# A fused macaron block: x normalised on ScalarE, its first low half through a product on TensorE, and a new order of all queues

## The chip, the cores and the metric

One core of a Trainium2 chip. The metric is the time of one execution on the device in microseconds; three runs of the kernel before gave 164.55, 164.68 and 165.19, median 164.68.

## What is computed

x has 1024 rows of 256 channels. A block of three residual steps, each on a layer-normalised copy of its input:

```python
x = x + 0.5 * ffn(layernorm(x), gate_w, up_w, down_w, gate_scale, up_scale, down_scale)
x = x + attn(layernorm(x), w_qkv, w_g, w_proj, gn_weight, gn_bias)
x = x + 0.5 * ffn(layernorm(x), ...)              # the same weights again

def ffn(h):                                       # weights rounded to float8_e4m3fn
    gate = silu((h @ q8(gate_w)) * gate_scale)    # 256 -> 768
    up = (h @ q8(up_w)) * up_scale
    return ((gate * up) @ q8(down_w)) * down_scale

def attn(h):                                      # 16 heads of 16 channels
    q, k, v = split(h @ w_qkv); q, k = xpos(q), xpos(k)
    y = (q @ k.T * decay_mask / 4) @ v            # no softmax
    return (silu(h @ w_g) * groupnorm(y)) @ w_proj
```

## The kernel before

Rows are worked on in 8 tiles of 128 (`NT`). In the two feedforward steps four tiles make a group of 512 columns (`GT`), and the 768 inner channels are six blocks: 12 gate/up products per step, numbered `j`; `PRODUCTS` orders those of the first step as blocks 0 to 2 of both groups, then 3 to 5 of both. Attention runs over 8 chunks of 128 rows with a running state.

There are no loops at run time. Each engine has one queue, written out by hand as calls of small functions, and engines meet only at semaphores; a function waits for what it reads and for the buffer that it writes. An instruction that waits holds up all behind it on its engine.

**Opening.** SyncE loads x in three parts (tiles 0 and 1, 2 and 3, 4 to 7) between the pieces of the weights. `tile_stats` and `mean_var` (VectorE) give mean and variance, `roots` (GpSimd, L309) the power -1/2 for a group of tiles, `shift_rows` (VectorE) minus mean times root. Even tiles are normalised by `norm_act` (ScalarE, L409) from that shift, odd ones by `norm_tile` (VectorE, L680). `turn_h` (TensorE, L1089) transposes four tiles into two PSUM banks. `split_h` (ScalarE, L417) copies a bank, scaled by 2^-90, to `hhi` in fp32r (a high half), and `rest_h` (VectorE, L692) writes what is lost, bank times 2^-90 minus `hhi`, to `hlo`. Products take both halves: `gate_up(j)` is four 128x512 matmuls for gate and four for up (L1125), `first_gate_up` the same for j = 0 (L1101). `keep_busy` are products of zeros.

**Weights.** Each of 8 pieces is rounded by `grid_step` (L613), `grid_clip` (L619), `grid_add` (L625) on VectorE, `subtract` on VectorE (L630) or GpSimd (L305, where `SUB_ON_POOL` names it), and `to_weights` (ScalarE, L401). Three buffers (`GRID_SLOTS`) are shared by turns. `PIECES_NEEDED` says how many pieces a product waits for; `down(0)` needs the seventh, its second half the eighth.

**First feedforward step.** Per product: `silu` (ScalarE, L427), `fuse_up` (VectorE, L709: up times scale times silu), `split_f` (ScalarE, L435) and `rest_f` (VectorE L717 or GpSimd L320, where `REST_ON_POOL` names it) give `fhi` and `flo`; `fuse` has four slots. `down(d)` multiplies them with the down weights for tile d (L1153), `scale_down` and `add_down` give x1. `turned_vectors` (VectorE) copies the scales that TensorE has transposed, `half_scale` halves the down scales.

**Attention, chunk c.** `norm_tile`, `turn_h2` (L1169), `copy_h2`; `project_qk` (L1181) and `project_vg` (L1192, L1195); `rotate_parts` (VectorE, L746) and `rotate` (L758, L759); `turn_qk` (L1207) and `copy_qk` (ScalarE: kT, qM, qT); `scores` (L1224) into four banks, `mask_scores(c, 0..3)` (VectorE, L766); `update_state` (L1261), `mask_kv`, `add_state`; `values` (L1240 and L1248); `copy_y`, `turn_y` (L1281), `group_mean` (L786, L790), `square` (ScalarE, L484), `group_var` (L798), `group_roots` (GpSimd, L336), `group_norm` (L804), `turn_gn` (L1294), `affine` (ScalarE, L492), `gated` (L812), `project_out` (L1304), `add_proj` (L816). `turn_qk(c+1)` and `turn_h2(c+2)` write banks of the scores of chunk c, so they wait for its first and second mask; `scores(c+1)` waits for all four, `values(c)` for each in turn.

In a full chunk TensorE's order is scores(c), project_out(c-3), project_vg(c+1), turn_h2(c+2), turn_gn(c-2), values(c), turn_y(c-1), turn_qk(c+1), update_state(c+1), project_qk(c+2). The last chunk is interleaved with the first products of the second feedforward step, whose second group (`turn_h(3)`) needs the last tile of the attention's output.

## Time and profile before

| | |
|---|---|
| runs | 164.55, 164.68, 165.19 us; median 164.68 |
| profiled execution | 164.07 us, span 162.3 us, mean granted TensorE clock 1.00 (2.4 GHz) throughout |
| chain that ended last, by engine | TensorE 62%, VectorE 16%, GpSimd 9%, issue 7%, DMA 2% |

The span runs from the first to the last instruction; 1.8 us of the execution lie around it. How to read the profile: PE is TensorE (its weight loads are PEld), DVE is VectorE, ACT ScalarE, POOL GpSimd, SP SyncE. An instruction's row gives its start, its length, engine, line, operation, output and inputs. The length of an instruction that waits for a port inside the engine includes that wait. Ends of matmuls are modelled, so that neighbours overlap in the rows: what a group takes from the queue is read from its start to the next one's.

### The profile page before, as it was taken

How to read it: one execution, taken by the hardware profiler on the slowest of the kernel's cores; microseconds unless marked ns; L12 is line 12 of the kernel's file. 1: busy time of each engine (PE TensorE's matmuls, PEld its weight loads, DVE VectorE, ACT ScalarE, POOL GpSimd, SP SyncE). 2: the span in 40 equal slices, each digit the busy share in tenths (PEclk: the TensorE clock that was granted, in tenths of full speed). 3: DMA queues.
4: the chain of work that ended last, by engine and by line, in shares of the span. 5: the costliest groups of instructions: out<-in, count | busy, mean ns of one | idle time of the engine just before them, and what ended most of it. 6: DMA issues, size and time to landing. Idle time of an engine off the chain costs nothing.

```text
span 162.3 us, 3236 instructions
## 1 busy us (share of the span) xinstructions
PE 151.5 (93%) x1111; PEld 117.6 (72%) x1111; DVE 134.0 (83%) x295; ACT 71.4 (44%) x158; POOL 70.5 (43%) x77
## 2 busy tenths in 40 slices
PE   5758699999999999999999999999999989999992
PEld 2335478787979785858686786668778768888991
DVE  1899799997787694879898999999898989657774
ACT  3235669953232214152608071354716718554300
POOL 2558569851376300256372737373567630000000
PEclk9999999999999999999999999999999999999999
DMA  4999501903000000000000000000000000000123
GB/s 111 288 306 338 203 2 24 360 7 129 2 0 4 0 0 4 0 0 0 6 0 0 6 0 0 4 0 2 4 0 2 4 0 0 0 0 0 67 69 129
DMA packets 6864, 8.41 MB, mean 52 GB/s; under 512 B 432, under 2 KB 5568, under 8 KB 6848
## 3 DMA queue, kind: packets, MB, share of 16 engines
q1 hardware_dynamic: 6848, 8.20, 15.1%
q8 instruction: 9, 0.15, 0.4%
q14 instruction: 7, 0.06, 0.1%
HBM read 7.15 MB, written 1.05 MB: 51 GB/s over the span
## 4 chain that ended last, share of the span: by engine, by line
PE 62%; DVE 16%; POOL 9%; issue 7%; DMA 2%; ACT 1%; SPq 1%; POOLq 0%; DVEq 0%
PE bank L1125 14%; PE bank L1153 12%; PE bank L1181 9%; POOL grstd L336 5%; PE bank L1224 4%; PE bank L1248 4%; PE bank L1192 3%; PE bank L1304 3%; PE bank L1195 3%; DVE flo L717 3%; DMA xt<-in_L_attn_x 2%; PE bank L1207 2%; PE bank L1261 2%; DVE raw L625 2%; POOL rstd L314 2%
## 5 line engine op out<-in xcount | busy, mean ns | idle before, releaser
L1125 PE MATMUL bank<-hh,gate_r 128*128 128x512 f32 x92 | 25.7, 401 | 0.2
L1125 PE MATMUL bank<-hh,up_r 128*128 128x512 f32 x92 | 25.7, 401 | 0.0
L1153 PE MATMUL bank<-down_r,fhi 128*128 128x256 f32 x96 | 24.2, 291 | 0.4 <-DVE flo L717 0.4
L336 POOL TENSOR_TENSOR grstd<-gve,neg_half 128x16 f32<-128x16 f32 x8 | 23.3, 2915 | 0.8 <-POOL gve L332 0.2
L1153 PE MATMUL bank<-down_r,flo 128*128 128x256 f32 x96 | 23.4, 282 | 0.0
L435 ACT ACTIVATE fhi<-fuse 128x512 fp32r<-128x512 f32 x24 | 14.8, 631 | 15.5 <-DVE fuse L709 15.5
L766 DVE TENSOR_TENSOR sc<-bank,msk 128x512 f32<-128x512 f32 x32 | 20.6, 682 | 0.6 <-PE bank L1224 0.6
L1125 PEld LDWEIGHTS bank<-hh,gate_r 128*128 128x128 f32 x92 | 16.8, 188 | 4.6 <-issue 1.2
L1125 PEld LDWEIGHTS bank<-hh,up_r 128*128 128x128 f32 x92 | 16.7, 189 | 4.2 <-issue 0.8
L709 DVE SCALAR_TENSOR_TENSOR fuse<-bank,vec,gact 128x512 f32<-128x512 f32 x24 | 17.6, 747 | 2.5 <-ACT gact L427 1.3
L427 ACT ACTIVATE gact<-bank,vec 128x512 f32<-128x512 f32 x24 | 16.1, 681 | 7.3 <-PE bank L1125 5.8
L1153 PEld LDWEIGHTS bank<-down_r,fhi 128*128 128x128 f32 x96 | 18.1, 189 | 1.3 <-DVE flo L717 0.8
L1153 PEld LDWEIGHTS bank<-down_r,flo 128*128 128x128 f32 x96 | 18.1, 189 | 0.5 <-issue 0.2
L312 POOL TENSOR_SCALAR ve<-mv 128x1 f32<-128x1 f32 (+3 forms) x15 | 4.4, 293 | 29.4 <-DVE mv L652 29.4
L492 ACT ACTIVATE ga<-bank,vec 128x128 f32<-128x128 f32 x16 | 6.5, 455 | 23.2 <-PE bank L1294 23.2
L1181 PE MATMUL bank<-wqkv,h 128*128 128x512 f32 x32 | 15.3, 599 | 0.0
L717 DVE TENSOR_TENSOR flo<-fuse,fhi 128x512 fp32r<-128x512 f32 x19 | 14.9, 794 | 0.1
L305 POOL TENSOR_TENSOR grid<-raw,grid 128x768 f32<-128x768 f32 (+2 forms) x6 | 10.5, 1763 | 7.7 <-DVE raw L625 7.7
L729 DVE TENSOR_TENSOR yd<-bank,ds 128x256 f32<-128x256 f32 x16 | 6.8, 423 | 7.4 <-PE bank L1153 7.3
L314 POOL TENSOR_TENSOR rstd<-ve,neg_half 128x1 f32<-128x1 f32 (+3 forms) x15 | 10.8, 721 | 1.3
L1304 PE MATMUL bank<-wp,go 128*128 128x256 f32 x32 | 8.8, 398 | 0.5 <-DVE go L812 0.4
L1224 PE MATMUL bank<-qM,kT 32*128 32x256 f32 x128 | 9.2, 400 | 0.0
(86 smaller groups left out, 279.7 us busy)
## 6 DMA issues: line engine op xcount, KB each, us to landing
raw<-in_rotation SPq DMA_DIRECT2D x1, 1536.0 KB, 6.7
out<-xt SPq DMA_DIRECT2D x8, 128.0 KB, 1.7
raw<-in_L_ffn_down_w SPq DMA_DIRECT2D x2, 384.0 KB, 7.7
wqkv<-in_L_attn_w_qkv SPq DMA_DIRECT2D x1, 768.0 KB, 9.1
xt<-in_L_attn_x SPq DMA_DIRECT2D x2, 256.0 KB, 3.3
xt<-in_L_attn_x SPq DMA_DIRECT2D x1, 512.0 KB, 5.9
raw<-in_rotation SPq DMA_DIRECT2D x1, 512.0 KB, 3.4
raw<-in_L_ffn_gate_w SPq DMA_DIRECT2D x1, 384.0 KB, 6.4
```

The source lines that it names most:

```text
L314: pool.tensor_tensor(rstd[:, a:b], ve[:, a:b], neg_half[:, 0:b - a], ALU.pow).then_inc(rstd_done, 1)
L336: pool.tensor_tensor(grstd[:, c % 2], gve[:, :], neg_half[:, :], ALU.pow).then_inc(grstd_done, 1)
L427: nc.scalar.activation(gact[:, j % 2, :], pairs[j // (NG * NI)][j % 2][0][:, :], ACT.Silu, scale=gate_col[:, i:i + 1]).then_inc(silu_done, 1)
L435: nc.scalar.activation(fhi[:, g % NG, i, :], fuse[:, j % FUSE_SLOTS, :], ACT.Copy).then_inc(fhi_done, 1)
L709: dve.scalar_tensor_tensor(out=fuse[:, j % FUSE_SLOTS, :], in0=pairs[j // (NG * NI)][j % 2][1][:, :], scalar=up_col[:, i:i + 1], in1=gact[ ...
L717: dve.tensor_tensor(flo[:, g % NG, i, :], fuse[:, j % FUSE_SLOTS, :], fhi[:, g % NG, i, :].bitcast(F32), ALU.subtract).then_inc(flo_dve, 1)
L766: dve.tensor_tensor(sc[:, r].rearrange("p k m t -> p (k m) t"), b_sc[r][:, :].rearrange("p (g t) -> p g t", t=P), causal.unsqueeze(1).to_b ...
L1125: mm = pe.matmul(dst[:, :], wr[m][:, k * I + i * P:k * I + (i + 1) * P], half[:, k, g % NG, :], start=(k == 0 and half is hhi), stop=(k == ...
L1153: mm = pe.matmul(downs[d][:, 0:C], half[:, g % NG, i, t * P:(t + 1) * P], wr["down"][:, i * C:(i + 1) * C], start=(i == 0 and half is fhi) ...
L1181: mm = pe.matmul(b_qk[:, :], h2[:, c % 2, k, :], wqkv[:, k, 0:2 * C], start=(k == 0), stop=(k == KC - 1))
L1224: mm = pe.matmul(b_sc[r][:, k * C:(k + 1) * C], kT[at, k, :], qM[at, k].rearrange("p m t -> p (m t)"), start=True, stop=True)
L1304: mm = pe.matmul(b_gn[c][:, C:2 * C], go[:, k, :], wp[:, k, :], start=(k == 0), stop=(k == KC - 1))
```

## The change

The opening: all eight tiles of x are normalised on ScalarE. For the first group the low half is no longer the work of VectorE. TensorE adds the product of a negated unit matrix (times 2^90, made by ScalarE from the unit matrix) with `hhi` to the transposed tiles in their bank, so that the bank holds x minus the high half, and ScalarE copies that to `hlo` (`low_h`). `first_gate_up` goes by k, with `take_high` ahead of each high product. `turned_vectors` and `half_scale` go from VectorE to ScalarE. `subtract(0)` and `subtract(6)` go to GpSimd and `subtract(3)` to VectorE; `rest_f` 0, 1, 2 and 11 go to VectorE and 3, 9 and 10 to GpSimd. `qT` gets a second buffer.

The order of every queue is new. In a full chunk of the attention TensorE's is scores(c), project_out(c-3), project_vg(c+1), turn_h2(c+2), update_state(c), turn_qk(c+1), turn_gn(c-2), project_qk(c+2), turn_y(c-1), values(c), and then scores(c+1). `down(7)` goes behind `scores(1)`, `project_vg(0)` ahead of `project_qk(0)`. In the last stretch `values(7)` comes two steps after `scores(7)` and `project_out(7)` one gate/up pair later.

```diff
+NORM_ON_ACT = [0, 1, 2, 3, 4, 5, 6, 7]
-SUB_ON_POOL = [1, 2, 3, 4, 5, 7]
+SUB_ON_POOL = [0, 1, 2, 4, 5, 6, 7]
-REST_ON_POOL = [0, 1, 2, 4, 11]
+REST_ON_POOL = [3, 4, 9, 10]
...
         @block.gpsimd
             roots(0)
+            subtract(0)
             roots(1)
             subtract(1)
             subtract(2)
-            subtract(3)
             roots(2)
             subtract(4)
-            rest_f(0)
             subtract(5)
-            rest_f(1)
-            rest_f(2)
+            subtract(6)
+            rest_f(3)
             rest_f(4)
             subtract(7)
...
         @block.scalar
+            def low_h(g, k):
+
+                act.wait_ge(high_taken, KC * g + k + 1)
+                nc.scalar.activation(hlo[:, k, g, :], turn[g][k][:, :], ACT.Copy, scale=H_SCALE).then_inc(hlo_done, 1)
...
+            to_weights(0)
             norm_act(0)
-            to_weights(0)
+            norm_act(1)
             norm_act(2)
+            negative_ident()
+            norm_act(3)
             split_h(0, 0)
+            turned_vectors()
+            to_weights(1)
             split_h(0, 1)
-            to_weights(1)
+            low_h(0, 0)
+            low_h(0, 1)
             to_weights(2)
             silu(0)
             to_weights(3)
             norm_act(4)
+            norm_act(5)
             norm_act(6)
+            norm_act(7)
             silu(1)
...
         @block.vector
             grid_clip(1)
-            norm_tile(1)
-            subtract(0)
             grid_step(2)
-            norm_tile(3)
+            shift_rows(1)
             grid_clip(2)
             grid_step(3)
-            shift_rows(1)
+            grid_add(1)
             grid_clip(3)
-            grid_add(1)
             grid_add(2)
             grid_add(3)
-            rest_h(0, 0)
             tile_stats(4)
-            rest_h(0, 1)
-            mean_var(4)
             tile_stats(5)
             tile_stats(6)
+            mean_var(4)
             tile_stats(7)
             mean_var(5)
             mean_var(6)
             mean_var(7)
-            turned_vectors()
+            subtract(3)
             grid_step(4)
             grid_step(5)
+            shift_rows(2)
             grid_clip(4)
-            shift_rows(2)
-            norm_tile(5)
-            norm_tile(7)
+            grid_clip(5)
             grid_add(4)
-            grid_clip(5)
+            grid_add(5)
             fuse_up(0)
...
             for c in range(2, 5):
-                mask_kv(c)
                 group_var(c - 2)
                 rotate_parts(c + 1)
                 mask_scores(c, 0)
                 mask_scores(c, 1)
-                mask_scores(c, 2)
+                rotate(c + 1)
                 if c >= 3:
                     add_proj(c - 3)
                 group_norm(c - 2)
+                mask_kv(c)
+                mask_scores(c, 2)
                 mask_scores(c, 3)
-                rotate(c + 1)
                 norm_stats(NT + c + 3, NT + c + 4)
+                gated(c - 2)
                 group_mean(c - 1)
-                gated(c - 2)
                 norm_tile(NT + c + 3)
...
         @block.tensor
+            def take_high(g, k):
+
+                pe.wait_ge(minus_done, 1)
+                pe.wait_ge(hhi_done, KC * g + k + 1)
+                pe.matmul(turn[g][k][:, :], minus[:, :], hhi[:, k, g, :], start=False, stop=True,
+                          skip_group_check=True).then_inc(high_taken, 1)
```

## Rows read from the trace of the kernel before

**Rows 1.** The page, part 1: busy time, share of the span and instructions.
```profile
PE 151.5 (93%) x1111; PEld 117.6 (72%) x1111; DVE 134.0 (83%) x295; ACT 71.4 (44%) x158; POOL 70.5 (43%) x77
```

**Rows 2.** Busy time by stretch: window, length, each engine (instructions), clock, DMA.
```profile
28.00:40.00 12.00, 11.65 (x62) 9.57 (x61) 11.06 (x16) 7.58 (x12) 6.37 (x5) 1.00 0.47 171
```

**Rows 3.** Timeline of the opening: start, length, instruction [idle before, releaser].
```profile
15.00 1.07 POOL L312 TENSOR_SCALAR ve<-mv 128x4 f32<-128x4 f32 x1 [0.57 <-DVE mv L652]
...
17.62 1.09 ACT L409 ACTIVATE h<-xt,shift,rstd 128x256 f32<-128x256 f32 x2 [1.28 <-DVE shift L637]
...
18.36 1.06 PE L1089 MATMUL bank<-msk,h 128*128 128x128 f32 x8 [1.23 <-ACT h L409]
...
22.32 1.10 PE L1125 MATMUL bank<-hh,up_r 128*128 128x512 f32 x4
```

**Rows 4.** Groups by form: count, busy us, mean ns of one, idle before.
```profile
L336 POOL TENSOR_TENSOR grstd<-gve,neg_half 128x16 f32<-128x16 f32 x8 | 23.3, 2915 | 0.8 <-POOL gve L332 0.2
...
L766 DVE TENSOR_TENSOR sc<-bank,msk 128x512 f32<-128x512 f32 x32 | 20.6, 682 | 0.6 <-PE bank L1224 0.6
...
L692 DVE SCALAR_TENSOR_TENSOR hh<-bank,hh 128x512 fp32r<-128x512 f32 x8 | 5.2, 684 | 0.0
...
L484 ACT ACTIVATE gsq<-gd 128x256 f32<-128x256 f32 x8 | 3.4, 426 | 2.7 <-DVE gd L790 2.7
...
L680 DVE TENSOR_SCALAR h<-xt,mv,rstd 128x256 f32<-128x256 f32 x4 | 1.6, 411 | 0.1
```

**Rows 5.** Timeline of GpSimd and VectorE where both read SBUF.
```profile
26.25 2.00 POOL L320 TENSOR_TENSOR flo<-fuse,fhi 128x512 fp32r<-128x512 f32 x1
...
27.03 1.77 DVE L717 TENSOR_TENSOR flo<-fuse,fhi 128x512 fp32r<-128x512 f32 x1
...
34.07 0.69 DVE L717 TENSOR_TENSOR flo<-fuse,fhi 128x512 fp32r<-128x512 f32 x1
...
34.23 2.23 POOL L305 TENSOR_TENSOR grid<-raw,grid 128x768 f32<-128x768 f32 x1 [2.29 <-DVE raw L625]
...
35.33 1.69 DVE L717 TENSOR_TENSOR flo<-fuse,fhi 128x512 fp32r<-128x512 f32 x1
```

**Rows 6.** Timeline of TensorE ahead of the second half of down(0).
```profile
35.89 1.10 PE L1125 MATMUL bank<-hh,gate_r 128*128 128x512 f32 x4
36.83 1.10 PE L1125 MATMUL bank<-hh,up_r 128*128 128x512 f32 x4
38.28 0.39 PE L1153 MATMUL bank<-down_r,fhi 128*128 128x256 f32 x1 [0.35 <-DVE flo L717]
```

**Rows 7.** Timeline of TensorE: two holes, and the same steps in a full chunk.
```profile
68.88 0.66 PE L1207 MATMUL bank<-msk,rot 128*128 128x128 f32 x4
69.67 0.68 PE L1261 MATMUL bank<-v,rot 128*128 128x128 f32 x4
...
74.93 0.38 PE L1169 MATMUL bank<-msk,h 128*128 128x128 f32 x2
75.58 0.44 PE L1294 MATMUL bank<-msk,gn 128*128 128x128 f32 x2 [0.26 <-DVE gn L804]
...
84.37 0.38 PE L1169 MATMUL bank<-msk,h 128*128 128x128 f32 x2
84.59 0.38 PE L1294 MATMUL bank<-msk,gn 128*128 128x128 f32 x2
...
86.67 0.60 PE L1207 MATMUL bank<-msk,rot 128*128 128x128 f32 x4
87.18 0.68 PE L1261 MATMUL bank<-v,rot 128*128 128x128 f32 x4
```

**Rows 8.** Timeline of TensorE: the scores of chunks 4 and 5.
```profile
89.51 1.15 PE L1224 MATMUL bank<-qM,kT 32*128 32x256 f32 x16
...
98.46 1.15 PE L1224 MATMUL bank<-qM,kT 32*128 32x256 f32 x16
```

**Rows 9.** Timeline of TensorE: the last projection of the attention.
```profile
130.88 1.13 PE L1304 MATMUL bank<-wp,go 128*128 128x256 f32 x4 [0.43 <-DVE go L812]
```

More of the change, by code:

```diff
@@ L83, in rests, with norms @@
     return n - on_pool, on_pool
-def normed_until(n):
-    return (n + 1) // 2 if n < NT else n + 1 - NT // 2
+def norms(n):
+    on_act = sum(t < n for t in NORM_ON_ACT)
+    return n - on_act, on_act
 def products_until(g, i):
@@ L1337, in _ @@
             down(4, 0, NI // 2)
+            project_vg(0)
             project_qk(0)
+            turn_h2(1)
             down(5, 0, NI // 2)
-            project_vg(0)
-            turn_h2(1)
             down(4, NI // 2)
             down(5, NI // 2)
+            down(6)
             turn_qk(0)
-            down(6)
             project_qk(1)
-            update_state(0)
-            down(7)
             scores(0)
@@ L1351, in _ @@
             turn_h2(2)
+            update_state(0)
             turn_qk(1)
+            project_qk(2)
             values(0)
-            project_qk(2)
             scores(1)
+            down(7)
+            turn_qk(2)
+            turn_h2(3)
+            update_state(1)
             turn_y(0)
-            update_state(1)
             project_vg(2)
-            turn_h2(3)
             values(1)
-            turn_qk(2)
-            update_state(2)
             project_qk(3)
+            scores(2)
             for c in range(2, 5):
-                scores(c)
                 if c >= 3:
@@ L1369, in _ @@
                 turn_h2(c + 2)
+                update_state(c)
+                turn_qk(c + 1)
                 turn_gn(c - 2)
+                project_qk(c + 2)
+                turn_y(c - 1)
                 values(c)
-                turn_y(c - 1)
-                turn_qk(c + 1)
-                update_state(c + 1)
-                project_qk(c + 2)
-            scores(5)
+                scores(c + 1)
+            update_state(5)
+            project_vg(6)
+            turn_h2(7)
             project_out(2)
-            project_vg(6)
+            project_qk(7)
             turn_gn(3)
-            turn_h2(7)
             turn_qk(6)
             turn_y(4)
-            project_qk(7)
             values(5)
+            scores(6)
+            update_state(6)
             project_out(3)
-            scores(6)
+            turn_qk(7)
             project_vg(7)
             turn_gn(4)
-            update_state(6)
-            turn_qk(7)
+            values(6)
             turn_y(5)
-            values(6)
+            scores(7)
             c, j0 = NT - 1, NG * NI
@@ L1396, in _ @@
             turn_y(c - 1)
-            scores(c)
+            values(c)
             project_out(c - 3)
+            turn_y(c)
             gate_up(j0, ("gate",))
             gate_up(j0, ("up",))
-            values(c)
+            turn_gn(c - 2)
             gate_up(j0 + 1, ("gate",))
-            turn_y(c)
-            turn_gn(c - 2)
             gate_up(j0 + 1, ("up",))
+            turn_gn(c - 1)
+            project_out(c - 2)
             gate_up(j0 + 2, ("gate",))
-            turn_gn(c - 1)
-            gate_up(j0 + 2, ("up",))
-            project_out(c - 2)
-            gate_up(j0 + 3, ("gate",))
             project_out(c - 1)
             turn_gn(c)
+            gate_up(j0 + 2, ("up",))
+            gate_up(j0 + 3, ("gate",))
+            project_out(c)
             gate_up(j0 + 3, ("up",))
-            project_out(c)
             gate_up(j0 + 4, ("gate",))
             gate_up(j0 + 4, ("up",))
+            turn_h(3)
             gate_up(j0 + 5, ("gate",))
-            turn_h(3)
             gate_up(j0 + 5, ("up",))
-            down(NT, 0, NI - 2)
             gate_up(j0 + 6, ("gate",))
```

357 lines of the change are left out of this document (189 added, 168 removed).

## The prediction

> **What bounds the kernel now.** I read the shares of busy time first: TensorE is busy 93% of the span, VectorE 83%, ScalarE 44%, GpSimd 43% [rows 1]. An average hides stages, so the table by stretch comes next: from 28 to 40 us TensorE has 11.65 of 12.00 us and VectorE 11.06 [rows 2]. From about 19 us on the kernel is a TensorE queue with a few holes, and VectorE is nearly full beside it. Work taken from VectorE is therefore worth only what it shortens of a hole in the TensorE queue; a reordering can close holes and can also open new ones.
>
> The holes are read from the starts of TensorE's groups, because the modelled ends of matmuls hide short ones. There are four kinds. (a) Before 19 us: TensorE idles 1.23 us until the second half of x is normalised [rows 3]. (b) Ahead of the second half of the first down product: the last gate/up group starts at 36.83 and the down product at 38.28, 1.45 us later, where the group before it took 0.94; about 0.52 us of hole, waiting for `flo` [rows 6]. (c) In the first attention chunks: `turn_qk(2)` at 68.88 to `update_state(2)` at 69.67 is 0.79, against 0.51 for the same step in a full chunk, so 0.28; and `turn_h2(4)` at 74.93 to `turn_gn(0)` at 75.58 is 0.65 against 0.22, so 0.43, waiting for `gn` [rows 7]. The full chunks run at TensorE's pace, without a hole: `scores(4)` starts at 89.51 and `scores(5)` 8.95 later [rows 8]. (d) In the last stretch: `project_out(7)` at 130.88 has 0.43 of idle time ahead of it, waiting for `go` [rows 9].
>
> **Opening.** The change takes from VectorE four normalisations (0.41 each), the two `rest_h(0, k)` (0.68 each) [rows 4], the three small `vec` instructions and `subtract(0)`; before the second half's statistics end that is about 1 us of its queue on the path, since part of the rest fell into waits for data. It adds to ScalarE four normalisations (two in a row took 1.09, so 0.6 for the first and 0.5 for each behind it), the two `low_h` and the negated unit matrix, and to TensorE two 128x512 products, about 0.23 each, a quarter of a gate/up group [rows 3, 6]. No row shows a ScalarE read of a bank to which an fp32r product has been added to transposes; the nearest are the 0.68 of VectorE's `rest_h`, which reads the same bank, and ScalarE's 0.5 for a tile half as wide; I take 0.6 each, bounds 0.5 and 0.8, hidden either way as follows.
>
> In the first half the new order of ScalarE is `to_weights(0)`, norms 0 and 1, norm 2, the unit matrix, norm 3. With roots and shifts where they are now or up to 0.5 us earlier, the fourth tile is turned between 10.4 and 11.0 us, and everything up to the gate product of `gate_up(2)` ends near 16.5. But none of this is last: `turn_h(1)` waits for tiles 4 to 7. Their statistics end about 1.0 us earlier (13.7 instead of 14.9, just ahead of the 15.00 of the first root instruction). Then two things take back: GpSimd's first instruction after them took 1.07 us, while two VectorE `grid_step`s ran beside it [rows 3], and in the new order `subtract(3)` and the same two steps stand there again; and all four norms stand in one row on ScalarE, four at 0.5 instead of two beside two. I get the shift at 16.45, norms from 16.65 to 18.75, and the last tile turned at 19.05 instead of 19.42 (18.36 and 1.06). `fuse_up(0)` now stands behind `grid_add(5)` on VectorE and ends at 20.0; the second up product waits for it, and `fuse_up(1)` at 21.95 releases the third, at 22.05 instead of 22.32 [rows 3]. So 0.27 us is left of the opening at that point. Bounds: 0.9 if the roots are not held up, 0 if the four norms end where they do now.
>
> **From 22 to 38 us.** The new plan moves `subtract(6)` and other `rest_f`s to GpSimd and takes `rest_f(0)` to `(2)` back to VectorE: VectorE's work between `fuse_up(2)` and `rest_f(8)` comes out nearly the same (two `rest_f` and a `fuse_up` more, a `subtract` and a `grid_add` less). 
>
> Walking the new queues with these prices: `grid_step(6)` waits 0.25 for `subtract(5)`, `rest_f(2)` 0.45 for `subtract(6)`, `grid_step(7)` 1.2 for `rest_f(3)`, `grid_add(7)` 0.45 for `rest_f(4)`, `rest_f(6)` 0.45 for `subtract(7)`: 2.8 us in all, as much as now. `rest_f(8)` ends at 37.9, the down product starts at 38.0 instead of 38.28. **Term 1 is -0.3 us**: the hole (b) goes, part of what the opening won goes with it. Bounds: without any new collision -1.25 (0.75 from the opening and 0.52 from the hole); if GpSimd's `rest_f(4)` slips in between `grid_step(7)` and `grid_clip(7)`, `fuse_up(6)` is 1.2 late, `up(8)` waits, and it is +0.5.
>
> The Trainium skill ("SBUF — State Buffer", who interferes with whom) says the same of the port pair: an exclusive lock, held for a whole instruction, against GpSimd, by VectorE instructions with two SBUF inputs as well as by its fast modes. It speaks against moving `subtract(0)` and `(6)` to GpSimd. The trace agrees for these operations, with the 1.77 and 1.69 above. If the powers (`rstd`) hold the pair for their whole length too, the last `shift_rows` and term 1 move by some tenths, to near 0.
>
> **First chunks.** `project_vg(0)` goes ahead of `project_qk(0)`, `down(7)` behind `scores(1)`, `update_state` one chunk later, `values(c)` directly ahead of `scores(c+1)`. I walked TensorE's new queue against the masks (0.68 each), the two rotation products (the same shape, taken at the same length) and the copies. `turn_qk(2)` has `down(7)` ahead of it and no longer waits: **term 2, -0.3**. `turn_gn(0)` stands 1.1 us further back, behind `update_state(2)` and `turn_qk(3)`, at about 4.2 us after `scores(2)` starts; the mean power of 2.9 us that feeds it has ended by then: **term 3, -0.4** [rows 4, 7]. Bounds for both together: -0.8 and 0.
>
> **Full chunks.** In a chunk that starts with `scores(c)` at S, `group_var(c-2)` at the head of VectorE's queue needs the square, which ScalarE does behind the copy of the values, which now end at S: 0.43 us each [rows 4], so the variance starts at S+0.85, not before S. Behind it wait the two rotation products to S+2.4, masks 0 and 1 to S+3.65, `rotate`, `add_proj` and `group_norm` to S+5.05. TensorE wants the second mask at S+3.80 (`turn_h2`), `rotate` at S+4.5, `gn` at S+5.0. The chunk stays at 8.95, with margins of 0.15 and 0.1. **Term 4, 0**; bounds 0 and +1.0 (0.34 in each of three chunks, if the first half of `rotate` takes twice the 0.33 that I take, beside an addition on GpSimd).
>
> **Last stretch.** `project_out(7)` stands behind one more gate/up pair, which closes (d), 0.43. In exchange `values(7)` has only `turn_h(2)` and `turn_y(6)` (1.25 us) between it and `scores(7)`, where VectorE needs four masks and a variance, 2.7 us or more: about 0.7 of a new hole; the gate product behind it waits 0.5 for `rest_h(2, 1)`, while holes of 0.1 to 0.2 at several places of today's order close. **Term 5, 0**; bounds -0.8 and +1.5. The tail after the last gate/up product is the same.
>
> **The sum**: -0.3 -0.3 -0.4 +0 +0 = -1.0 us. The profiled execution took 164.07 us, 162.3 of it span and 1.8 around it; it becomes 163.1. It lies 0.6 under the median of the runs, 164.68, so the forecast for the median is 163.7.
>
> **Rivals.** (A) As above: 163.7, own range 163.1 to 164.3, chance 0.38. (B) The opening's gain arrives whole, since the collisions fall otherwise than I walked them: term 1 is -1.25, which gives 162.7; for it speaks that the opening takes so much from VectorE; against it, that it is full in [rows 2] and that the four norms stand in a row. Chance 0.22. (C) The GpSimd instruction takes the lock between `grid_step(7)` and `grid_clip(7)`: term 1 is +0.5, the time 164.5; chance 0.20. (D) Slower: what stands behind the values on VectorE comes too late. It has a margin of 0.15 us; beyond it each tenth costs a tenth in each of three chunks, and the same chain runs over the end, where `group_var(3)`, `mask_scores(5, 1)` and `turn_y(4)` wait in a row. Priced at 1.0 (chunks) and the upper bound of term 5 (1.5), minus 0.3 of overlap, it gives 163.7 + 2.2 = 165.9. It decides from about 0.5 us of lateness per chunk. Chance 0.14. (E) The change doesn't do what it says: the negated product doesn't shorten the opening, since ScalarE with its eleven more instructions is last there; terms 2 and 3 stay, 164.0 to 164.3; chance 0.06.
>
> **Chances.** About 0.5% (0.8 us) is what a measurement of this kernel can tell from no change. Under 163.9 lie two thirds of A (0.27), B (0.22) and a little of E: 0.50. Over 165.5 lies D: 0.14. The rest, 0.36, is no difference. The range that leaves 2 in 10 out goes from the middle of B, 162.3, to 165.1, past C.
>
> **What would show it.** Right: the last transpose of `turn_h(1)` ends near 19.0; the first product of the second half of `down(0)` starts at 37.8 to 38.1 with VectorE still full ahead of it; `scores(4)` starts about 1.5 us earlier than 89.51 (0.5 of it because its `update_state` now comes behind it); scores stand 8.95 apart. Wrong: `turn_h(1)` done before 18.6 (B), an `up` product that waits over 0.5 us for `fuse` between 28 and 36 us (C), chunks over 9.3 us (D), or a first half that is turned later than 11.4 (E).

## The result

Before, the runs beside which the changed kernel was timed had a median of 164.22 us (163.32 to 165.86). The changed kernel's median is 162.81 us (162.08 to 164.07): ratio 0.992, 95% interval 0.990 to 0.994, 1.4 us faster. A second timing of the same kernel gave 162.37 us and 0.990 (0.988 to 0.993). The forecast was 1.0 us less than before, 163.7 with a range of 162.3 to 165.1. The profiled spans are 162.3 and 161.0 us, a difference of 1.3. Of all runs named below, one that took 249.46 us at a mean granted clock of 0.57 (order in two halves, first kernel) and one of 165.51 us (its reverse) lie outside and are in no ratio.

From the page of the changed kernel, busy time and the chain that ended last, to be held against [rows 1]:

```profile
PE 152.3 (95%) x1113; PEld 118.8 (74%) x1113; DVE 131.2 (81%) x285; ACT 75.5 (47%) x169; POOL 69.8 (43%) x77
...
PE 73%; DVE 13%; issue 4%; DMA 4%; SPq 3%; POOL 1%; ACT 0%; DVEq 0%; ACTq 0%
```

VectorE has 2.8 us less to do, ScalarE 4.1 more, and TensorE fills 95% of a shorter span. The opening, from the timeline of the changed kernel (start, length, engine, line, instruction, idle time before and what ended it), answers to [rows 3]:

```profile
13.59 1.00 POOL L315 TENSOR_SCALAR ve<-mv 128x4 f32<-128x4 f32 x1 [1.26 <-DVE mv L687]
...
16.15 2.08 ACT L412 ACTIVATE h<-xt,shift,rstd 128x256 f32<-128x256 f32 x4 [1.40 <-DVE shift L672]
16.89 1.83 PE L1102 MATMUL bank<-msk,h 128*128 128x128 f32 x8 [1.38 <-ACT h L412]
...
18.71 0.74 DVE L730 SCALAR_TENSOR_TENSOR fuse<-bank,vec,gact 128x512 f32<-128x512 f32 x1
...
20.61 1.09 PE L1148 MATMUL bank<-hh,gate_r 128*128 128x512 f32 x4
...
21.54 1.11 PE L1148 MATMUL bank<-hh,up_r 128*128 128x512 f32 x4
```

`turn_h(1)` ends at 18.72 instead of 19.42, although its four tiles now come one by one, 0.5 apart, and its products are strung over 1.83 us. The third up product (of block 3 in the order of `PRODUCTS`, `up(3)`) starts at 21.54 instead of 22.32: the opening brought 0.78 there. From 27 to 38 us part of it was lost. The same timeline:

```profile
27.61 3.31 POOL L323 TENSOR_TENSOR flo<-fuse,fhi 128x512 fp32r<-128x512 f32 x2
...
28.12 1.66 DVE L648 TENSOR_SCALAR grid<-raw 128x768 uint32<-128x768 uint32 x1
...
29.81 1.53 DVE L654 TENSOR_SCALAR grid<-grid 128x768 f32<-128x768 f32 x1
30.63 1.09 PE L1148 MATMUL bank<-hh,gate_r 128*128 128x512 f32 x4
31.25 0.74 DVE L730 SCALAR_TENSOR_TENSOR fuse<-bank,vec,gact 128x512 f32<-128x512 f32 x1
...
32.14 1.17 PE L1148 MATMUL bank<-hh,up_r 128*128 128x512 f32 x4 [0.42 <-DVE fuse L730]
33.38 1.16 PE L1148 MATMUL bank<-hh,gate_r 128*128 128x512 f32 x4
...
37.90 0.28 PE L1176 MATMUL bank<-down_r,fhi 128*128 128x256 f32 x1
```

GpSimd runs `rest_f(3)` and `rest_f(4)`. VectorE's `grid_step(7)` waits for the first of them (1.66) and `grid_clip(7)`, behind it, for the second (1.53; where nothing runs beside it, 0.55). So `fuse_up(6)` ends at 31.99, `up(8)` starts 1.51 after its gate product instead of 0.93, and the next group 1.24 later instead of 0.94. The hole (b) of [rows 6], 0.52, is gone, and holes of 0.58, 0.30 and 0.06 ahead of 32.14, 33.38 and 34.38 have come. With the same work between, it is 16.36 us from the third up product to the second half of `down(0)`, 15.96 before; that half starts at 37.90, against 38.28.

From there on I compare the starts of the scores. Before, they lie at 56.86, 63.52, 72.00, 80.57, 89.51, 98.46, 108.30 and 115.71; after, at 54.73, 61.63, 70.81, 78.59, 87.48, 96.49, 106.54 and 113.40. `update_state(c)`, 0.52 us, used to stand ahead of `scores(c)` and now stands behind it; from `scores(2)` on the work ahead is otherwise the same. Allowing for it, the lead over before is 0.67 us at `scores(2)`, 1.46 at `scores(3)`, 1.45 at `scores(5)` and 1.3 at the end of the span, and the differences are the terms of the table below. The first full chunk, TensorE, to be held against the rows of a full chunk in [rows 7]:

```profile
73.74 0.38 PE L1192 MATMUL bank<-msk,h 128*128 128x128 f32 x2
73.96 0.61 PE L1284 MATMUL bank<-v,rot 128*128 128x128 f32 x4
...
74.41 0.60 PE L1230 MATMUL bank<-msk,rot 128*128 128x128 f32 x4
74.84 0.38 PE L1317 MATMUL bank<-msk,gn 128*128 128x128 f32 x2
75.06 1.88 PE L1203 MATMUL bank<-wqkv,h 128*128 128x512 f32 x4
```

There is no hole in front of `turn_gn(0)` (0.43 before), and `turn_qk` takes 0.43 from start to next start where it took 0.51. The end, TensorE:

```profile
96.49 1.15 PE L1247 MATMUL bank<-qM,kT 32*128 32x256 f32 x16
...
100.50 0.41 PE L1192 MATMUL bank<-msk,h 128*128 128x128 f32 x2 [0.46 <-DVE sc L787]
...
104.65 0.41 PE L1304 MATMUL bank<-msk,yT 128*128 128x128 f32 x2 [0.51 <-issue]
...
116.16 2.38 PE L1271 MATMUL bank<-sc,v 128*32 128x128 f32 x32
```

Idle times of 0.46 and 0.51 stand between `scores(5)` and `scores(6)`; from start to next start the first hole is 0.63 (1.52 from the second group of `project_vg(6)` to `turn_h2(7)`, 0.89 in a full chunk) and the second about 0.6. `values(7)` takes 2.38 instead of 1.12, since it waits for its masks.

| term | forecast | profiled, after less before |
|---|---|---|
| 1, to the second half of `down(0)` | -0.3 | -0.38 |
| 2, hole at `turn_qk(2)` and its surroundings | -0.3 | -0.29 |
| 3, hole at `turn_gn(0)` and its chunk | -0.4 | -0.79 |
| 4, full chunks | 0 | +0.01 |
| 5, behind `scores(5)` | 0 | +0.15 |
| sum | -1.0 | -1.30 |

### The profile page after: what moved, and what is told of

Its sections match the earlier page's. It is cut to its first block, busy times and chain, and to the rows that moved or that the text cites. A ratio compares the mean times of both kernels' runs of the same rounds, so it can differ in the third digit from the quotient of the medians.

```text
span 161.0 us, 3249 instructions
## 1 busy us (share of the span) xinstructions
PE 152.3 (95%) x1113; PEld 118.8 (74%) x1113; DVE 131.2 (81%) x285; ACT 75.5 (47%) x169; POOL 69.8 (43%) x77
## 4 chain that ended last, share of the span: by engine, by line
PE 73%; DVE 13%; issue 4%; DMA 4%; SPq 3%; POOL 1%; ACT 0%; DVEq 0%; ACTq 0%
PE bank L1148 18%; PE bank L1176 13%; PE bank L1203 9%; PE bank L1271 5%; PE bank L1247 5%; PE bank L1327 5%; PE bank L1215 4%; DMA xt<-in_L_attn_x 4%; PE bank L1218 4%; DVE fuse L730 2%; PE bank L1230 2%; PE bank L1284 2%; PE bank L1263 2%; DVE grid L648 1%; PE bank L1192 1%
## 5 line engine op out<-in xcount | busy, mean ns | idle before, releaser
L1176 PE MATMUL bank<-down_r,fhi 128*128 128x256 f32 x96 | 23.7, 285 | 0.0
L738 DVE TENSOR_TENSOR flo<-fuse,fhi 128x512 fp32r<-128x512 f32 x20 | 14.0, 717 | 3.1 <-ACT fhi L461 3.0
L308 POOL TENSOR_TENSOR grid<-raw,grid 128x768 f32<-128x768 f32 (+2 forms) x7 | 12.0, 1723 | 9.1 <-DVE raw L660 9.1
L468 ACT ACTIVATE h<-bank 128x256 f32<-128x256 f32 x8 | 3.1, 385 | 26.0 <-PE bank L1192 26.0
L315 POOL TENSOR_SCALAR ve<-mv 128x1 f32<-128x1 f32 (+3 forms) x15 | 5.0, 332 | 15.5 <-DVE mv L687 15.5
L347 POOL TENSOR_TENSOR state<-state,kvm 128x256 f32<-128x256 f32 x6 | 4.4, 728 | 15.6 <-DVE kvm L797 13.9
L317 POOL TENSOR_TENSOR rstd<-ve,neg_half 128x1 f32<-128x1 f32 (+3 forms) x15 | 10.3, 687 | 1.2
L1271 PE MATMUL bank<-sc,v 128*32 128x128 f32 x256 | 10.2, 277 | 0.0
```

Source lines behind the costliest of these rows:

```text
L308: pool.tensor_tensor(packed(grid, q), piece(raws[PIECES[q][0]], q), packed(grid, q), ALU.subtract).then_inc(sub_pool, 1)
L317: pool.tensor_tensor(rstd[:, a:b], ve[:, a:b], neg_half[:, 0:b - a], ALU.pow).then_inc(rstd_done, 1)
L738: dve.tensor_tensor(flo[:, g % NG, i, :], fuse[:, j % FUSE_SLOTS, :], fhi[:, g % NG, i, :].bitcast(F32), ALU.subtract).then_inc(flo_dve, 1)
L1176: mm = pe.matmul(downs[d][:, 0:C], half[:, g % NG, i, t * P:(t + 1) * P], wr["down"][:, i * C:(i + 1) * C], start=(i == 0 and half is fhi) ...
L1271: mm = pe.matmul(b_y[r * 2 * D:(r + 1) * 2 * D, k * P:(k + 1) * P], v2[:, c % 2, hd, :], sc[:, r, k, m, :], start=(c == 0 and m == 0), sto ...
```

## The experiments

Eleven new kernels were run, and the changed one again, all beside runs of the kernel before (medians 164.05 to 164.22 us). A distance inside one execution is quoted to 0.01 us; the medians move by a few tenths, for two reasons shown further down: the landing of transfers, and the clock that TensorE was granted. A diff is against the changed kernel where nothing else is said.

**The order in two halves.** First the changed opening and order up to `down(3)`, with the order of before behind it. At the join, VectorE:

```diff
             fuse_up(11)
             norm_tile(NT + 1)
             scale_down(3)
             rest_f(11)
+            mean_var(NT + 2)
             rotate_parts(0)
+            rotate(0)
             scale_down(4)
-            rotate(0)
 ...
```

> The changed kernel's order up to the end of down(3) and the last of the first feedforward step (its opening with the product of the negated unit matrix included), and from there every queue as before (qT keeps its second buffer). Theory (the gain has two independent parts, one of 0.4 us up to the second half of down(0), the rest from the attention's order): 0.3 to 0.5 us faster than before, ratio 0.9970 to 0.9982, and the starts of the scores keep the old distances. Rival (the opening alone carries the gain, what follows only passes it on): 1.0 to 1.4 us faster, ratio 0.992 to 0.994.

Measured: 164.77 us, ratio 1.003 (1.001 to 1.005), no gain at all. The opening is there (`turn_h(1)` ends at 18.86). But the timeline has a wait that neither kernel has:

```profile
46.18 1.27 POOL L323 TENSOR_TENSOR flo<-fuse,fhi 128x512 fp32r<-128x512 f32 x1
...
46.25 1.34 DVE L701 TENSOR_SCALAR h<-x,mv,rstd 128x256 f32<-128x256 f32 x1
47.52 0.41 DVE L750 TENSOR_TENSOR yd<-bank,ds 128x256 f32<-128x256 f32 x1
...
48.08 0.36 PE L1176 MATMUL bank<-down_r,fhi 128*128 128x256 f32 x1 [0.96 <-DVE yd L750]
```

The old order wants `down(5)` early, and its bank is freed by `scale_down(3)`, which in the new order stands behind `norm_tile(9)`; that one waits 0.9 us for GpSimd's `rest_f(10)`. So this kernel says nothing of the opening. It was run again with the two lines exchanged:

```diff
             fuse_up(11)
-            norm_tile(NT + 1)
             scale_down(3)
+            norm_tile(NT + 1)
             rest_f(11)
```

> The kernel with the changed order up to down(3) and the order of before behind it, with scale_down(3) now ahead of norm_tile(9) on VectorE. In the first form of that kernel scale_down(3) stood behind norm_tile(9), which waits for a power on GpSimd, and TensorE waited 0.96 us for it in front of down(5). Theory (the opening is worth its 0.3 to 0.7 us alone, and the join hid it): that wait is under 0.2 us, the span from the end of turn_h(1) is 0.8 to 1.0 us shorter than in the first form (163.1 less 18.86), the ratio to the kernel before is 0.995 to 0.998. Rival (the old order behind is fitted to the old arrival, and the wait shows up in another place): the ratio stays at 1.000 to 1.003 and a wait of 0.5 us or more stands somewhere in the distances of the first four scores. All of the computation is made.

Measured: 163.36 us, ratio 0.994 (0.992 to 0.996), span 161.5. The wait is gone, and from the end of `turn_h(1)` (18.48) to the end of the span it takes 143.0 us instead of 144.2, in the kernel before 142.9. So the whole gain of this kernel lies ahead of that point. The medians differ by 0.69 us, the upper end of the 0.3 to 0.7 of the first theory; the ratio is a little better than its range.

Then the reverse, the old order up to `down(3)` and the new one behind it (its diff is the other half of the change; its opening is that of [rows 3]):

> The kernel before up to the end of down(3), with its opening, and from there every queue as in the changed kernel (second buffer of qT). Theory (independent parts): 0.8 to 1.0 us faster than before, ratio 0.994 to 0.995; scores(2) to scores(3) takes 7.8 us, not 8.57. Rival (the new attention order is worth nothing without the earlier start): no change. Second rival (the parts feed each other): faster than the whole change minus its first part by more than 0.3 us either way.

Measured: 163.41 us, ratio 0.996 (0.994 to 0.999), span 161.4. `scores(2)` to `scores(3)` takes 7.78 us, as expected; the medians differ by 0.64, less than the 0.8 to 1.0 of the theory, the profiled spans by 0.9. The two halves alone are worth 0.6% and 0.4%; together they make the 0.8% to 1.0% of the whole. Within these intervals they add.

**The last stretch.** The changed kernel up to `scores(5)` and `update_state(5)`, and the old order behind. TensorE:

```diff
             update_state(5)
-            project_vg(6)
-            turn_h2(7)
             project_out(2)
+            project_vg(6)
+            turn_gn(3)
+            turn_h2(7)
-            project_qk(7)
-            turn_gn(3)
             turn_qk(6)
 ...
```

> The changed kernel up to scores(5) and update_state(5), and from there every queue as before. In the trace the stretch from scores(5) to the end takes 0.15 us longer in the changed kernel than in the one before (holes at turn_h2(7), turn_y(4) and inside values(7)), so theory (the new end is a small loss): 0.0 to 0.3 us faster than the changed kernel, 1.3 to 1.6 us faster than before. Rival (the new end is fitted to the state in which the new chunks leave the queues): the old end is up to 0.5 us slower than the changed kernel.

Measured: 164.72 us, ratio 1.005 (1.003 to 1.008), the opposite of what I expected. Its timeline:

```profile
98.33 0.41 DVE L819 TENSOR_REDUCE gvar<-gsq 128x16 f32<-128x256 f32 x1
...
99.11 2.91 POOL L339 TENSOR_TENSOR grstd<-gve,neg_half 128x16 f32<-128x16 f32 x1
...
102.06 0.42 DVE L825 TENSOR_TENSOR gn<-gd,grstd 128x256 f32<-128x256 f32 x1 [0.21 <-POOL grstd L339]
...
102.54 0.44 PE L1317 MATMUL bank<-msk,gn 128*128 128x128 f32 x2 [1.97 <-DVE gn L825]
```

The new chunks hand over with `group_var(3)` not yet done; the old end wants `turn_gn(3)` as its third step and waits 1.97 us for a 2.91 us power. From `scores(5)` to the end of the span it takes 66.34 us, in the changed kernel 64.51. Less the one wait it would be 64.37, an estimate: this kernel was not mended at its join as the one above was, so it says that an end belongs to the chunks ahead of it, and does not price term 5.

**The low half on VectorE.** Of the opening's edits, one undone: `hlo` of the first group is again made by `rest_h(0, k)` on VectorE, without the negated matrix and its two products.

```diff
             grid_add(3)
+            rest_h(0, 0)
             tile_stats(4)
+            rest_h(0, 1)
             tile_stats(5)
 ...
-                            take_high(0, k)
+                            pe.wait_ge(hhi_done, k + 1)
```

> The changed kernel, but the low half of the first group is VectorE's again (the two rest_h, the first ahead of tile_stats(4), the second behind it), without the negated unit matrix, the two products and the two copies. Theory (VectorE's chain of tile_stats(4) to (7), roots, shift and then its full queue up to the hole ahead of the up product of block 8 is what the opening is bound by): all of it moves by 0.6 to 0.7 us, the kernel is 0.5 to 0.7 us slower than the changed one. Rival (the collisions with GpSimd between 27 and 31 us swallow the opening's gain, so its parts are worth nothing): within 0.15 us of the changed kernel. What speaks for the rival: the changed kernel had won 0.78 us at the third up product and only 0.38 at the down product.

Measured: 164.43 us, ratio 1.002 (1.000 to 1.004), 1.6 to 2.1 us over the two medians of the changed kernel and not 0.6. Part of it is TensorE's clock. The table by stretch (window, length, busy time of TensorE, its weight loads, VectorE, ScalarE, GpSimd, then granted clock, DMA share, GB/s):

```profile
16.00:18.00 2.00, 0.04 (x1) 0.07 (x2) 1.07 (x4) 0.78 (x2) 0.99 (x1) 1.00 0.99 379
18.00:20.00 2.00, 1.89 (x10) 1.14 (x11) 2.00 (x4) 2.00 (x5) 0.93 (x1) 1.00 0.45 158
20.00:22.00 2.00, 2.00 (x7) 1.51 (x6) 2.00 (x4) 2.00 (x5) 2.00 (x2) 0.51 0.00 0
22.00:24.00 2.00, 2.00 (x8) 1.56 (x7) 1.48 (x3) 0.74 (x2) 1.35 (x1) 0.63 0.00 0
```

TensorE had stood idle for 2.00 us ahead of `turn_h(1)`, and from 20.0 to 23.3 us it was granted the lower of its two levels, 1.2 GHz instead of 2.4: the eight up products from 19.54 took 3.34 us where they take 2.30 in the changed kernel. So the idle time was filled, with all else left as it was:

```diff
+            keep_busy(4)
             turn_h(1)
```

> The earlier kernel whose first low half is made on VectorE, with four products of zeros of 0.27 us each put in front of turn_h(1) on TensorE, where that engine stood idle for 2.00 us from 15.96 to 17.96, and where afterwards the granted clock was 0.51 from 20 to 22 us and 0.63 from 22 to 24. Theory (of the 2 us that the low half on VectorE cost, about 1.6 was the clock, which fell because TensorE had stood idle): the granted clock stays 1.00 from 14 to 26 us, the eight products up of line 1148 take what they do in the changed kernel and not 3.34, gate(3) starts 0.7 to 1.2 us behind its place in the changed kernel and not 2.07, and the span is 161.0 to 161.6. Rival (the low half's own chain on VectorE is what costs 2 us: the products of the second half wait for it): the clock may or may not be 1.00, but the groups stay long by waits, and the span is 162.4 to 162.8. All of the computation is made, and four products of zeros besides.

Measured: 163.78 us, ratio 0.996 (0.994 to 0.999), by the medians 0.65 us better for four products of zeros. The same table of this kernel:

```profile
16.00:18.00 2.00, 2.00 (x10) 1.45 (x8) 1.07 (x4) 0.61 (x2) 1.26 (x2) 1.00 1.02 388
...
20.00:22.00 2.00, 2.00 (x10) 1.42 (x9) 2.00 (x4) 2.00 (x5) 2.00 (x2) 1.00 0.00 0
22.00:24.00 2.00, 2.00 (x10) 1.51 (x9) 2.00 (x4) 1.95 (x4) 1.75 (x1) 1.00 0.00 0
```

The clock stays up, as the theory says; the span is 162.4 and not 161.0 to 161.6, as the rival says. Neither is all of it. Counted from the first `ve`, the third up product starts 9.30 us later without the filling, 7.93 with it and 7.95 in the changed kernel: behind the statistics the clock was the whole difference, 1.4 us at that point. Not all of that reaches the end: from the end of `turn_h(1)` to `scores(0)` it takes 36.63 us without the filling, 35.98 with it and 36.01 in the changed kernel, so 0.65 is left, as in the medians, and the rest went into waits that were there anyway. The single run of the unfilled kernel in which the mean clock stayed at 1.00 took 163.77 us, the median of the filled one. The other part of the loss lies ahead of the statistics: the two `rest_h`, 0.6 each from start to next start, stand in front of the statistics, and `ve` comes at 15.03 instead of 13.59. Of that 1.44, 1.2 is the two instructions; the other 0.2 is what the landings of the weights and of x differ by, below.

**The four norms in a row.** In the changed kernel, norms 5 and 7 on VectorE again:

```diff
-NORM_ON_ACT = [0, 1, 2, 3, 4, 5, 6, 7]
+NORM_ON_ACT = [0, 1, 2, 3, 4, 6]
 ...
             shift_rows(2)
+            norm_tile(5)
+            norm_tile(7)
             grid_clip(4)
```

> The changed kernel with two of the four normalisations of the second group of tiles (5 and 7) on VectorE again, in front of grid_clip(4), the others on ScalarE. Theory (four normalisations in a row on ScalarE, 2.08 us together, set the end of turn_h(1), so halving them brings it forward; but VectorE then hands over the first products later): turn_h(1) ends 0.7 to 1.0 us sooner behind the first normalisation than in the changed kernel (2.57 us from 16.15 to 18.72), gate(3) starts at most 0.3 us sooner, since fuse_up(0) and rest_h(1, *) stand 1.1 to 1.7 us later on VectorE; the ratio is within 0.004 of the changed kernel's. Rival (TensorE's start of the second group is all that counts): gate(3) starts 0.7 us sooner and the kernel is 0.5 us faster than the changed one. All of the computation is made.

Measured: 163.27 us, ratio 0.993 (0.991 to 0.996). Its timeline:

```profile
15.75 1.09 ACT L412 ACTIVATE h<-xt,shift,rstd 128x256 f32<-128x256 f32 x2 [0.77 <-DVE shift L670]
...
16.50 1.07 PE L1102 MATMUL bank<-msk,h 128*128 128x128 f32 x8 [0.68 <-ACT h L412]
...
18.96 0.74 DVE L728 SCALAR_TENSOR_TENSOR fuse<-bank,vec,gact 128x512 f32<-128x512 f32 x1
...
19.85 1.18 PE L1148 MATMUL bank<-hh,up_r 128*128 128x512 f32 x4 [1.36 <-DVE fuse L728]
```

`turn_h(1)` ends 1.82 us behind the first norm instead of 2.57, as expected, and it is worth nothing, less even than the theory allowed (gate(3) at most 0.3 sooner): `fuse_up(0)` stands 0.7 later on VectorE, counted from the first norm, TensorE waits 1.36 us for the bank that it frees, and gate(3) starts 5.12 behind the first norm instead of 4.46. So with these two norms in it VectorE's queue, not the turning of the tiles, is what the opening's path runs through. What moving them brings is under the noise of the medians (0.991 to 0.996 against 0.990 to 0.994); in the traces, counted from the landing of the gate weights (below), `scores(0)` starts 47.17 us behind it here and 46.46 in the second profile of the changed kernel.

**The collision and the masks.** One move on VectorE takes `fuse_up(6)` from behind the pair of waits:

```diff
             grid_step(7)
-            grid_clip(7)
             fuse_up(6)
+            grid_clip(7)
             grid_add(7)
```

> The changed kernel with one step moved: fuse_up(6) on VectorE between grid_step(7) and grid_clip(7), not behind both. In the changed kernel grid_step(7) took 1.66 us and grid_clip(7) 1.53 us instead of 0.55, beside GpSimd's rest_f(3) and rest_f(4), and the up product of block 8 waited for fuse_up(6), which could have run from 29.7. Theory (the hole is made of these two waits for the other engine's whole instruction; fuse_up, with an input in PSUM, passes): fuse_up(6) ends 1.5 us earlier, the hole of 0.5 us ahead of that up product goes, 0.5 to 0.7 us faster than the changed kernel. Rival (VectorE's sum up to rest_f(8) is what binds, and the down product waits for it): the hole moves to down(0), under 0.15 us of gain.

Measured: 161.94 us, ratio 0.987 (0.985 to 0.989). The changed kernel, run beside it, had 162.37. From the end of `turn_h(1)` to `scores(0)` it takes 35.43 us instead of 36.01 in both profiles of the changed kernel, the 0.58 of the hole. The timeline:

```profile
28.06 1.65 DVE L648 TENSOR_SCALAR grid<-raw 128x768 uint32<-128x768 uint32 x1
29.66 0.75 DVE L730 SCALAR_TENSOR_TENSOR fuse<-bank,vec,gact 128x512 f32<-128x512 f32 x1
30.32 0.97 DVE L654 TENSOR_SCALAR grid<-grid 128x768 f32<-128x768 f32 x1
...
31.52 1.10 PE L1148 MATMUL bank<-hh,up_r 128*128 128x512 f32 x4
```

`fuse_up(6)`, with an operand in PSUM, runs its usual 0.75 beside GpSimd's `rest_f(4)`, and the clip pays only the rest of that (0.97 instead of 1.53). Holes of 0.32 and 0.08 stay two and three groups behind `up(8)`, much as the 0.30 and 0.06 of the changed kernel; they are not the work of this pair of waits. Another move takes the hole ahead of `turn_h2(7)` (0.46 idle, 0.63 from start to next start):

```diff
             mask_scores(5, 0)
+            mask_scores(5, 1)
             tile_stats(16)
             mask_kv(5)
             rotate(6)
-            mask_scores(5, 1)
```

> The changed kernel with mask_scores(5, 1) directly behind mask_scores(5, 0) on VectorE, ahead of tile_stats(16), mask_kv(5) and rotate(6). Theory (turn_h2(7) waits for this mask, 0.63 us of hole): the hole goes, turn_y(4) behind it keeps its own of 0.5; 0.4 to 0.6 us faster. Rival (the chain over affine(3) to turn_y(4) or the one over group_roots at the end is as late, and takes it back): under 0.15 us.

Measured: 162.27 us, ratio 0.989 (0.986 to 0.992); `scores(5)` to `scores(6)` 9.40 instead of 10.05. The gain is seen in the trace alone: the median is only 0.1 under the 162.37 of the changed kernel beside it. These two with a third, the variance of chunk 5 behind all four masks of `scores(7)`:

```diff
             mask_scores(c, 0)
-            group_var(c - 2)
             mask_scores(c, 1)
             mask_scores(c, 2)
             mask_scores(c, 3)
+            group_var(c - 2)
```

> The changed kernel with l1's and m1's moves and a third one: group_var(5) behind the four masks of chunk 7, since values(7) stood over these masks for 1.26 us more than in a full chunk. If the moves add: 0.9 to 1.4 us faster than the changed kernel, 2.2 to 2.7 faster than before. If the last stretch is bound by the three powers of 2.9 us in a row on GpSimd: the third move costs up to 0.3.

Measured: 162.98 us, ratio 0.992 (0.990 to 0.995). The first two moves are in it to the hundredth (35.41 and 9.40), and the third costs 1.6, not the 0.3 at most of the second theory: from `turn_h(2)` to `turn_h(3)` it takes 19.62 instead of 18.00. GpSimd, its own timeline:

```profile
116.53 2.92 POOL L339 TENSOR_TENSOR grstd<-gve,neg_half 128x16 f32<-128x16 f32 x1
...
120.05 2.90 POOL L339 TENSOR_TENSOR grstd<-gve,neg_half 128x16 f32<-128x16 f32 x1
...
123.56 2.95 POOL L339 TENSOR_TENSOR grstd<-gve,neg_half 128x16 f32<-128x16 f32 x1
```

Three powers stand in a row, 3.5 apart, and the third releases `turn_gn(7)`. They stand in a row in the changed kernel too, but there the first starts 2.62 us behind `scores(7)`, here 4.41; a late start of the first shifts all three. The hole in `values(7)` that the move was to close hardly shrank (2.16 from start to next start instead of 2.32). Without the third move:

> The changed kernel with the two moves that paid when each was made alone: fuse_up(6) between grid_step(7) and grid_clip(7) (it brought scores(0) 0.58 us nearer to turn_h(1)), and the second half of the masks of scores(5) ahead of tile_stats(16), mask_kv(5) and rotate(6) (scores(5) to scores(6) 0.65 us shorter). Theory (both holes are on the path that sets the end, and they add): distance from the end of turn_h(1) to scores(0) 35.4, scores(5) to scores(6) 9.40, span from the end of turn_h(1) to the last instruction 141.0 to 141.2; median 1.2 us under the changed kernel, ratio to the kernel before near 0.985. Rival (what the first move brings is taken by waits of the chunks, as the cheaper steps were): span from the end of turn_h(1) 141.6 and the ratio near 0.988. All of the computation is made.

Measured: 161.59 us (161.10 to 161.82), ratio 0.982 (0.979 to 0.985), span 159.3, and from the end of `turn_h(1)` 141.0 us, as the theory says. It is the fastest of all, 2.5 us under the kernel before and 0.8 to 1.2 under the changed one.

**The changed kernel again.**

> The changed kernel once more, beside the three below on one chip: 0.9921 of before, as measured, within 0.002.

Measured: 162.37 us, ratio 0.990 (0.988 to 0.993), span 160.5, 0.5 less than in its first profile. All of the 0.5 lies in the opening: `turn_h(1)` ends at 18.27 instead of 18.72, and everything behind it takes 142.2 or 142.3 us. The rows of the two executions on VectorE, first the second, then the first:

```profile
7.82 0.44 DVE L648 TENSOR_SCALAR grid<-raw 128x512 uint32<-128x512 uint32 x1 [0.45 <-DMA raw<-in_L_ffn_gate_w]
...
11.38 0.74 DVE L683 BATCH_NORM_STATS2 stats<-xt 128x6 f32<-128x256 f32 x2
```

```profile
7.46 0.43 DVE L648 TENSOR_SCALAR grid<-raw 128x512 uint32<-128x512 uint32 x1 [0.19 <-DMA raw<-in_L_ffn_gate_w]
...
11.82 0.43 DVE L683 BATCH_NORM_STATS2 stats<-xt 128x6 f32<-128x256 f32 x1 [0.62 <-DMA xt<-in_L_attn_x]
```

In the first profile the second half of x had not landed when VectorE came to it; in the second it had. Counted from the landing of the gate weights (read as the start of the `grid_step` that waits for them, the first row of each), the end of `turn_h(1)` comes 11.50 us later with the old opening (two kernels) and 10.43 to 10.54 with the new one in six kernels whose statistics don't wait for x; with such a wait it is 10.79 to 11.26, in three. So the change's opening is worth up to 1.06 us, of which x's transfer takes back 0.3 to 0.8 in some executions.

The second thing that moves the medians is the clock. Of the 35 runs of the kernel before that stood beside the first experiments, 26 had a mean granted clock of 1.00 and a median of 163.92 us, nine had 0.99 and 164.76. Of the 18 of the changed kernel, 14 had 1.00 and 162.65, four 0.99 and 163.90. The ratio of the runs at 1.00 is the 0.992 of all, so the change's gain does not come from this. It does bear on the halves: at 1.00 the mended first half has 163.36 (all 12 runs) and the second 163.19 (7 of 12), 0.6 and 0.7 under the kernel before; their sum is the 1.3 of the whole.

## Why the prediction was right, and where it was not

**What bounds the kernel.** Holds. TensorE is busier in a shorter span, and both moves that paid closed a hole in its queue. The kernel with two norms on VectorE is the clearest: TensorE got its tiles sooner and waited for `fuse_up(0)` instead.

**Term 1, -0.3 against -0.38,** is right in its sum by luck, two errors that cancel. The opening's term was mis-sized: 0.37 at the end of `turn_h(1)`, measured 0.70, and up to 1.06 counted from the landing. The statistics ended where forecast (13.7, `ve` at 13.59), but only because 0.62 of waiting for x is in them; without it `ve` is at 13.14. That x's second half is the next thing to be late I had not named. The step that failed is the next one, from there to the shift: with a hold-up of the roots added I put the shift at 16.45, 2.75 us later; it came at 15.95, 2.36 later, and before it took 2.42 (15.00 to 17.42), so the hold-up was in the base already and I charged it twice. The four norms in a row and the two `low_h` (0.63 and 0.60) took what I gave them. Of the gain 0.4 was then given back between 28 and 35 us (holes of 0.94 came, one of 0.52 closed), 0.58 of it by the mechanism of rival C, GpSimd between `grid_step(7)` and `grid_clip(7)`. Its sign, an up product that waits over 0.5 us, was met (0.58 from start to next start); its lateness of 1.2 was too high, since the clip took 0.98 more than alone. The move of `fuse_up(6)` shows that this was the cause of the 0.58; what makes the 0.36 behind it was not tried. The chances should not have set B and C against each other: the opening came in as large as B's 0.75, and C's collision came as well.

**Term 2** is right in size; it was not tried alone. **Term 3** is mis-sized (-0.79 for -0.4): the hole of 0.43 closed as said, but the chunk gained 0.36 more, since in it five of the same steps took less than before (last section). **Term 4** is right: 8.89 and 9.01 against 8.94. The 0.3 that the first full chunk had gained is lost again in these two: from the second group of `project_vg` to `project_qk` it takes 2.45 and 2.57 us instead of 2.21 (81.50 to 83.95, 90.39 to 92.96, 72.85 to 75.06), spread over all the steps between. The margins of 0.1 that I walked may be the reason; no run shows it. **Term 5** is right in its sum (+0.15) and in place for `values(7)`, but again by cancelling: 1.26 of waits there against 0.7 forecast, and some 1.2 ahead of `turn_h2(7)` and `turn_y(4)` that I had not priced, against more gains than I had named. The hole (d) closed as said; what stands between `turn_gn(7)` and `project_out(7)` is now two products where one stood, so the projection comes behind seven products of the second feedforward step and not, as said ahead, one pair later than before (it was behind eight). Whether the new end by itself is the small loss of 0.15 stays open: the old end behind the new chunks is 1.8 us worse, counted from `turn_h(1)`, but that is the one wait at its join.

**The rivals.** By the time itself, 162.81 lies under A's own range (163.1 to 164.3) and close to B's 162.7. Half of that is the base: the 18 runs beside the changed kernel have a median of 164.22, the three that I started from 164.68. Taken by the change against before, -1.4 lies within A's own range of -1.6 to -0.4 and between A (-1.0) and B (-2.0). B's sign, `turn_h(1)` done before 18.6, was missed in the first profile (18.72) and met in the second (18.27), so it turns on how the transfers land. C's mechanism came, its time did not. D (chunks over 9.3) did not come: 9.01 at most up to `scores(5)`. E did not: undoing the negated product alone costs 1.0 to 1.4 us by the medians even where the clock stays up (163.78 against 162.81 and 162.37), and the first half was turned at 9.93, sooner than the 10.4 to 11.0 that I walked.

## What to carry over

Before you price work taken from a queue, look at what each engine waits for next, transfers included, and where the partner on the same port will get in between two dependent instructions; here an instruction that reads PSUM, put between them, cost nothing. A new order of one stage cannot be judged with an old order behind it until the join has been looked at in the trace: here one exchange of two lines was worth 1.2 us and turned the verdict round. Where TensorE stands idle just ahead of a bound stretch (here for 2 us), look at the granted clock behind it, and at the mean clock of every run, not of the profiled one alone: here 0.99 instead of 1.00 went with 0.6 to 1.3 us, at most as much as the whole change brought.

## What the runs showed of the hardware

**The same step has several prices.** From start to next start, in the first full chunk of the changed kernel `update_state` took 0.45, `turn_qk` 0.43, `turn_gn` 0.22, `project_qk` 1.72 and `turn_y` 0.22; in the kernel before they took 0.52, 0.51, 0.27 (behind its wait), 1.81 and 0.28 in the same chunk, 0.35 us more in all. Two of these stay so in every full chunk of each kernel: `project_qk` 1.81 ahead of the scores and 1.72 ahead of `turn_y`, `turn_y` 0.28 ahead of `turn_qk` and 0.22 ahead of the values. The others don't go with the neighbour: in the next two chunks of the changed kernel, in the same order, `update_state` took 0.51 and 0.52 and `turn_qk` 0.51 and 0.55. Why was not tried.
